# The state layer of an eight-layer kernel: its recurrence inputs summed up spread over the partitions in PSUM, its states read in place, its gate as a tangent, and four row sums in another order

## The chip, the cores and the metric

The kernel runs on one core of one Trainium2 chip, as one launch. The time is device microseconds of that core for the whole program, all eight layers in one go. Kernels are compared by the median of several runs.

## The reference

Sixteen sequences of 256 tokens with 128 features (4096 tokens) go through eight residual layers: cosine attention, a mixture of 160 experts, a gated linear recurrence, the mixture again, the state layer, a feed-forward layer, rotary attention, and the feed-forward layer again. Each is `x = x + f(layernorm(x))`. All is float32. The change is in the fifth, the state layer:

```python
def _L1_attn_a_ref(x, W_in, b_in, conv_w, conv_b, A, C, Dp, W_out, b_out):
    x_and_z = x @ W_in + b_in
    x_proj, z = jnp.split(x_and_z, 2, axis=-1)          # 256 channels each
    xc = causal_conv(x_proj, conv_w)                    # 4 taps for each channel
    x_conv = xc + conv_b
    def step(h, xt):
        h = jnp.tanh(xt @ A + h)                        # 16 states for each sequence
        yt = h @ C.T + Dp * xt
        return (h, yt)
    _, ys = scan(step, 0, x_conv)                       # over the 256 tokens
    return (sigmoid(z) * ys) @ W_out + b_out
```

The scan is the awkward part: a hyperbolic tangent of the sum of this token's input and the last token's state can't be regrouped, so each sequence takes 256 steps one after the other.

## The kernel before, in words

The residual stream `X` stays in SBUF for the whole program as 32 tiles of 128 tokens (partition = token). Every layer goes over it in 8 steps (`STEPS`) of 4 tiles (`TPI`), 512 tokens (`W`), which are two whole sequences. The five engines run instruction streams of their own and meet at semaphores: VectorE (DVE), ScalarE (ACT), TensorE (PE), GpSimd (POOL) and SyncE (SP, which only starts DMAs). Between layers 5, 6, 7 and 8 there is a barrier (`finish`): all compute engines drain and wait for one another. Layers 2, 3, 4 and 5 have none.

The mixture of experts ahead of the state layer leaves its results in DRAM rows (`slot_results`). POOL fetches them back, 8 indirect DMAs for each tile (L1779), into a ring `GATHERED` of four tile places; DVE adds them into `X`, 8 weighted additions for each tile (`sum_rows`, L1749). Tile t+4 is fetched only when tile t has been added. The second half of the tiles (16 to 31) is fetched and added while the state layer already works on the first half, so `mamba_vector` carries these 16 tile sums between its own work; `front(i)` makes sure that the four tiles of step i have been summed.

The state layer (`mamba_*`, lines 832 to 1016) goes, for each step i:
- `front`: DVE takes mean and variance (L573, L577), ACT the square root (`deviations`, L177, which needs its own activation table), DVE the reciprocal (L181) and the normalised rows `XN` (L590), PE transposes them (L602), ACT copies them to `XT` (L934).
- PE multiplies by `W_in` (L993, four matmuls of 128x512), ACT adds the bias to the first half (`XP`, L938) and takes the sigmoid of the second (`Z`, L941).
- DVE does the four taps of the convolution into `XCS` (`convolve`, L900 and L902, 8 instructions).
- ACT copies it into `XC` for the whole layer (L943). PE multiplies by `A` to 16 rows x 512 columns in PSUM bank 5 (L998), and ACT copies that to `U16` (L945), on 16 partitions.

The recurrence (`recur`) works on 8 sequences at once, a group g: 8 sequences x 16 states are 128 partitions, and each token is one ACT instruction on a column of 128x1 (L955, L952 for the first), whose bias is the column before. To bring `U16` from 16 partitions to 128, SP starts 8 small DMAs for each group (`spread`, L973); to bring the states back to 16 partitions for the multiplication by `C`, another 8 (`collect`, L978). Group 0 (steps 0 to 3) is done in four parts of 64 tokens, one behind each of ACT's steps 4 to 7; group 1 follows behind step 7 in one go.

The output (`output(i)`): PE multiplies the states by `C` (L1003, 2 matmuls with 16 rows and 512 columns), DVE adds `D * XC` (L914), multiplies by the gate (L917) and adds the bias to `X` (L919), PE multiplies by `W_out` (L1010, 8 matmuls), DVE adds the result to `X` (L923). The outputs of group 0 run beside the recurrence of group 1; those of group 1 come after it, then the barrier.

The feed-forward layer behind it takes a sigmoid too (L790), inside a hardware loop of 7 rounds and once after it. Loads of activation tables are put in by the compiler, in the program's order, ahead of each function that the table in place doesn't have.

## Time and profile before

| | us |
|---|---|
| median of 3 runs | 2880.16 |
| lowest, highest | 2865.74, 2882.03 |
| the profiled execution, whole time | 2874.02 |
| its span, from first to last instruction | 2872.2 |
| state layer, from its first DVE instruction (1772.36) to the first of the next layer (2169.56) | 397.2 |

Busy shares of the span: PE 60%, DVE 49%, ACT 34%, POOL 38%. The mean clock that TensorE was granted is 0.723 of full speed. The page's first lines give such shares for the whole program; they say little about one layer. For this change the timeline of the state layer, engine by engine, is what is read: each row has a start time from the span's start, how long the row's instructions took together, the engine, the line, what is written from what, how many instructions, and in brackets how long the engine stood idle before it and what ended the wait. "PEld" are weight loads of TensorE.

### The profile page before, as it was taken

To read this page: it belongs to the slowest core of one execution; us is meant where nothing else is said; L and a number is where in the kernel's file an instruction comes from. 1 tells how busy PE (TensorE), PEld (TensorE's weight loads), DVE (VectorE), ACT (ScalarE), POOL (GpSimd) and SP (SyncE) were. 2 spreads that over 40 slices of the span, in tenths; PEclk is the share of its full clock that TensorE was granted. 3 is DMA by queue.
4 is the path that set the end of the run, shared out by engine and by line. 5 is a ranking of instruction groups with operands and counts; after the bars stand their busy time and mean duration, and the time that the engine had idled before them with its cause. 6 is when DMAs were issued, how large, how long until landed. Compare 5 with 4: busy or idle time off the path is not lost.

```text
span 2872.2 us, 40719 instructions
## 1 busy us (share of the span) xinstructions
PE 1731.2 (60%) x13716; PEld 1131.0 (39%) x13716; DVE 1404.3 (49%) x3650; ACT 970.4 (34%) x1719; POOL 1077.8 (38%) x1177
## 2 busy tenths in 40 slices
PE   4765424777676453465676766422426488888965
PEld 2544313555454232243555544100214334554543
DVE  3648833222434677676222444633215466766644
ACT  3651102333233321321332333356842223443342
POOL 2100777743751774765743762770001200000000
PEclk9985556888877655656887887655555568998985
DMA  8990116998996111115998996110000000000001
GB/s 234 327 388 23 48 51 207 320 315 273 324 289 216 52 52 46 51 57 171 321 318 274 327 308 202 50 52 2 4 2 0 0 1 1 1 1 1 1 1 30
DMA packets 294225, 383.68 MB, mean 134 GB/s; under 512 B 70816, under 2 KB 163696, under 8 KB 293872
## 3 DMA queue, kind: packets, MB, share of 16 engines
q1 hardware_dynamic: 177280, 160.91, 17.8%
q10 hardware_dynamic: 83984, 153.13, 15.4%
q0 software_dynamic: 32768, 67.17, 7.3%
q8 instruction: 108, 1.77, 0.2%
q14 instruction: 85, 0.70, 0.1%
HBM read 231.64 MB, written 175.11 MB: 142 GB/s over the span
## 4 chain that ended last, share of the span: by engine, by line
PE 38%; DVE 17%; DMA 13%; ACT 11%; issue 9%; POOL 6%; SPq 4%; DVEq 0%; ACTq 0%; POOLq 0%
DMA arena<-expert_blocks 11%; ACT arena L955 5%; PE psum L1984 5%; PE psum L1974 5%; POOL slot_rows L1768 4%; PE psum L448 3%; PE psum L1947 3%; SPq L1866 3%; PE psum L1347 2%; PE psum L1328 2%; PE psum L432 2%; PE psum L993 1%; PE psum L427 1%; ACT arena L1210 1%; PE psum L815 1%
## 5 line engine op out<-in xcount | busy, mean ns | idle before, releaser
L1779 POOL DMA_INDIRECT arena<-slot_results,SLOTS x512 | 492.3, 962 | 429.9 <-DMA slot_results<-arena 239.0
L1768 POOL DMA_INDIRECT slot_rows<-arena,SLOTS x512 | 512.0, 1000 | 332.4 <-issue 332.4
L1738 DVE COPY arena<-psum 128x512 f32<-128x512 f32 x288 | 197.2, 690 | 632.3 <-PE psum L1984 615.6
L1974 PE MATMUL psum<-arena 128*64 128x128 f32 x2304 | 233.0, 334 | 229.7 <-DMA arena<-expert_blocks 208.0
L1822 ACT ACTIVATE arena<-psum 128x512 f32<-128x512 f32 x288 | 172.0, 597 | 475.7 <-PE psum L1947 435.8
L169 POOL TENSOR_SCALAR rstd<-mv 128x4 f32<-128x4 f32 x32 | 6.2, 195 | 774.6 <-DVE mv L577 774.1
L1947 PE MATMUL psum<-ident,arena 128*128 128x128 f32 x1152 | 224.7, 328 | 72.7 <-DMA arena<-slot_rows 72.1
L1974 PEld LDWEIGHTS psum<-arena 128*64 128x64 f32 x2304 | 148.8, 163 | 296.6 <-DMA arena<-expert_blocks 226.3
L1984 PE MATMUL psum<-arena 64*128 64x128 f32 x2304 | 249.0, 345 | 7.3 <-DVE arena L1738 7.2
L1984 PEld LDWEIGHTS psum<-arena 64*128 64x128 f32 x2304 | 186.2, 226 | 70.4 <-issue 69.7
L1829 ACT ACTIVATE arena<-psum 128x256 f32<-128x256 f32 x288 | 110.6, 384 | 271.7 <-PE psum L1974 268.9
L1749 DVE SCALAR_TENSOR_TENSOR X<-arena,WEIGHTS,X 128x128 f32<-128x128 f32 x512 | 180.1, 352 | 41.0 <-DMA arena<-slot_results,SLOTS 25.1
L1947 PEld LDWEIGHTS psum<-ident,arena 128*128 128x128 f32 x1152 | 145.8, 163 | 117.0 <-issue 80.9
L955 ACT ACTIVATE arena<-arena 128x1 f32<-128x1 f32 x510 | 150.0, 294 | 16.6
L602 PE MATMUL psum<-ident,XN 128*128 128x128 f32 x192 | 45.3, 382 | 174.3 <-DVE XN L590 169.9
L1101 DVE TENSOR_REDUCE arena<-psum 128x1 f32<-128x128 f32 x256 | 74.1, 289 | 101.5 <-PE psum L1347 96.7
L1210 ACT ACTIVATE arena<-psum 128x1536 f32<-128x1536 f32 x64 | 92.8, 1450 | 80.1 <-PE psum L432 80.1
L602 PEld LDWEIGHTS psum<-ident,XN 128*128 128x128 f32 x192 | 34.0, 201 | 204.9 <-issue 193.4
L1102 DVE TENSOR_REDUCE arena<-psum 128x1 f32<-128x256 f32 x256 | 105.8, 413 | 0.0
L448 PE MATMUL psum<-arena 128*32 128x256 f32 (+1 forms) x1536 | 93.5, 349 | 8.6 <-ACT arena L1210 5.3
L427 PE MATMUL psum<-arena 51*128 51x256 bf16 (+1 forms) x384 | 64.7, 285 | 40.3 <-ACT arena L349 22.7
L448 PE MATMUL psum<-arena,ones 128*32 128x256 f32 (+1 forms) x1536 | 88.7, 335 | 0.0
(245 smaller groups left out, 3132.8 us busy)
## 6 DMA issues: line engine op xcount, KB each, us to landing
arena<-slot_rows ACTq DMA_DIRECT2D x288, 256.0 KB
slot_results<-arena ACTq DMA_DIRECT2D x288, 256.0 KB
arena<-expert_blocks SPq DMA_DIRECT2D x512, 96.0 KB
arena<-own_blocks SPq DMA_DIRECT2D x160, 256.0 KB
slot_rows<-zeros SPq DMA_DIRECT2D x2, 18432.0 KB, 79.5
own_blocks<-in_expert_w SPq DMA_DIRECT2D x4, 2560.0 KB, 22.6
slot_rows<-arena,SLOTS POOLq DMA_INDIRECT x512, 2.2
arena<-slot_results,SLOTS POOLq DMA_INDIRECT x512
```

Source lines behind the costliest of these rows:

```text
L448: mm = pe.matmul(psum[32 * r:32 * r + 32, 3, 256 * half + lo:256 * half + hi], ones4[:, head_of(n, r) % 4, :] if half else vp(kt, head_of( ...
L955: act.activation(H[:, g, t:t + 1], U[:, g, t:t + 1], ACT.Tanh, bias=H[:, g, t - 1:t]).then_inc(m_h[g], 1)
L1210: act.activation(PR2[:, g % 2], psum[:, 4:8, 0:384], ACT.Exp, scale=DH ** -0.5).then_inc(r_exp.sem, 1)
L1738: dve.tensor_copy(YSB[:, p].rearrange("p (c h) d -> p h c d", h=2), psum[:, first:first + 2, 0:256].rearrange("p h (c d) -> p h c d", c=2) ...
L1749: dve.scalar_tensor_tensor(X[:, t, :], GATHERED[:, j, k], WEIGHTS[:, t, k:k + 1], X[:, t, :], ALU.mult, ALU.add).then_inc(g_sum.sem, 1)
L1768: pool.indirect_dma_start(out=slot_rows[h], out_offset=bass.IndirectOffsetOnAxis(ap=slots_of(t, k), axis=0), in_=XNH[:, t], in_offset=None ...
L1779: pool.indirect_dma_start(out=GATHERED[:, t % TPI, k], out_offset=None, in_=slot_results[h], in_offset=bass.IndirectOffsetOnAxis(ap=slots_ ...
L1822: act.activation(XSBT[:, g % UNROLL], psum[:, g % 2, :], ACT.Copy).then_inc(c_xt.sem, 1)
L1829: act.activation(HEB[:, g % 2], psum[:, 2 + 5 * (g % 2), 0:256], ACT.Silu).then_inc(c_he.sem, 1)
L1947: mm = pe.transpose(psum[:, p % 2, P * q:P * q + P], XSB[:, p, q], ident[:])
L1974: mm = pe.matmul(psum[lo:lo + INTER, 2 + 5 * (p % 2), o:o + P], gate_of(g, q), XSBT[:, p, P * q:P * q + P], start=True, stop=True, skip_gr ...
L1984: mm = pe.matmul(psum[:, 3 + 2 * (p % 2) + q % 2, c:c + P], HEB[lo:lo + INTER, p % 2, c:c + P], down_of(g, q), start=True, stop=True, skip ...
```

## The change

Seven edits, all in the state layer.

1. The multiplication by `A` uses a wide stationary matrix. `A_AT[:, q, e, :]` is 128x128, zero but for the 16 columns of sequence q. Four matmuls for each step (2 sequences x 2 channel halves, 256 columns each) add into one PSUM bank for each group, banks 5 and 6, so that the inputs of 8 sequences come out on 128 partitions. `U16`, its copy and `spread` go.
2. ACT copies 128x256 from PSUM to `U` once for each group, in `recur`, ahead of the first token.
3. `C_AT` is the same for `C`: 128 rows with the 16 of sequence q filled, loaded by 8 DMAs from DRAM. PE multiplies it with `H` where it lies. `H16` and `collect` go; PE waits on the recurrence's own semaphore.
4. DVE clears and fills these matrices (`spread_out`) ahead of `front(0)`.
5. The gate: `sigmoid(z) = (1 + tanh(z/2)) / 2`. ACT takes the tangent with scale 0.5 and half the bias (`B_HALF`); DVE multiplies by `1 + Z` in one instruction, and the last addition scales by 0.5.
6. The 16 tile sums stand elsewhere: steps 0 to 3 have one each, behind the convolution; steps 4 to 6 have four each, two ahead of it and two behind.
7. Group 0's recurrence is in parts of 64, 96 and 96 tokens behind ACT's steps 4, 5 and 6; step 7 has none. PE's loops are written out.

```diff
-        m_ct = weight("m_ct", [STATE, E2, P])
-        U16 = view([STATE, NSEQ, SEQ])
+        HALF = NSEQ // 2
+        A_AT = view([P, HALF, E2, P])
+        C_AT = view([P, HALF, E2, P])
+        B_HALF = view([P, 2 * E2])
...
             def convolve(i):
-                dve.wait_ge(m_u_ps.sem, m_u_ps.before(0, i))
+                if i:
+                    dve.wait_ge(m_u_ps.sem, m_u_ps.before(0, i))
...
+            def spread_out():
+                dve.memset(C_AT, 0.0).then_inc(m_at, 1)
+                dve.memset(A_AT, 0.0).then_inc(m_at, 1)
+                dve.tensor_scalar(B_HALF, b_in[:], 0.5, None, ALU.mult).then_inc(m_at, 1)
+                dve.wait_ge(m_at, 2)
+                for q in range(HALF):
+                    dve.tensor_copy(A_AT[:, q, :, STATE * q:STATE * q + STATE], m_a[:]).then_inc(m_at, 1)
+            spread_out()
             front(0)
-            for i in range(STEPS - 2):
-                step(i, [TILES // 2 + 2 * i], [TILES // 2 + 2 * i + 1])
-            step(STEPS - 2, [TILES - 4, TILES - 3], [TILES - 2, TILES - 1])
+            for i in range(HSTEPS):
+                step(i, [], [TILES // 2 + i])
+            for i in range(HSTEPS, STEPS - 1):
+                step(i, [TPI * i + TPI, TPI * i + TPI + 1], [TPI * i + TPI + 2, TPI * i + TPI + 3])
...
-                    dve.tensor_tensor(ym(e), ym(e), Z[:, e, bass.ds(i * W, W)], ALU.mult).then_inc(m_ym.sem, 1)
+                    dve.scalar_tensor_tensor(ym(e), Z[:, e, bass.ds(i * W, W)], 1.0, ym(e), ALU.add, ALU.mult).then_inc(m_ym.sem, 1)
...
-                    act.activation(Z[:, e, bass.ds(i * W, W)], psum[:, 1 + E2 + e, :], ACT.Sigmoid, bias=b_in[:, E2 + e:E2 + e + 1]).then_inc(m_xp.sem, 1)
+                    act.activation(Z[:, e, bass.ds(i * W, W)], psum[:, 1 + E2 + e, :], ACT.Tanh, scale=0.5, bias=B_HALF[:, E2 + e:E2 + e + 1]).then_inc(m_xp.sem, 1)
...
-                act.wait_ge(m_u_ps.sem, m_u_ps.at(0, i))
-                act.activation(U16[:, bass.ds(i * 2, 2), :], psum[0:STATE, 5, :].rearrange("p (b q) -> p b q", b=2), ACT.Copy).then_inc(m_u.sem, 1)
...
                     if t == 0:
-                        act.wait_ge(m_spread, 16 * HALF * (g + 1))
+                        act.wait_ge(m_u_ps.sem, m_u_ps.at(0, HSTEPS * g + HSTEPS - 1))
+                        act.activation(U[:, g, :], psum[:, 5 + g, 0:SEQ], ACT.Copy).then_inc(m_h[g], 1)
+                        act.wait_ge(m_h[g], 1)
...
-            for k in range(STEPS // 2):
-                step(STEPS // 2 + k)
-                recur(0, part * k, part * k + part)
+            for k, steps in enumerate((64, 96, 96)):
+                step(HSTEPS + k)
+                recur(0, t, t + steps)
+                t += steps
+            step(STEPS - 1)
             recur(1, 0, SEQ)
...
+            sp.wait_ge(m_at, 1)
+            for q in range(HALF):
+                sp.dma_start(C_AT[STATE * q:STATE * q + STATE, q], a["m_ct"]).then_inc(m_ct, 16)
...
-                for e in range(E2):
-                    mm = pe.matmul(psum[0:STATE, 5, :], m_a[:, e, :], XCS[:, e].rearrange("p b q -> p (b q)"), start=(e == 0), stop=(e == E2 - 1))
+                for b in range(2):
+                    q = 2 * (i % HSTEPS) + b
+                    for e in range(E2):
+                        mm = pe.matmul(psum[:, 5 + i // HSTEPS, 0:SEQ], A_AT[:, q, e, :], XCS[:, e, b, :], start=(q == e == 0),
+                                       stop=(q == HALF - 1 and e == E2 - 1), skip_group_check=True)
...
                 for e in range(E2):
-                    mm = pe.matmul(psum[:, 1 + e, :], m_ct[:, e, :], H16[:, bass.ds(i * 2, 2), :].rearrange("p b q -> p (b q)"), start=True, stop=True)
+                    for b in range(2):
+                        mm = pe.matmul(psum[:, 1 + e, SEQ * b:SEQ * b + SEQ], C_AT[:, 2 * (i % HSTEPS) + b, e, :], H[:, i // HSTEPS, :],
+                                       start=True, stop=True, skip_group_check=True)
...
+            pe.wait_ge(m_ct, 16 * HALF)
+            pe.wait_ge(m_xp.sem, m_xp.end(0))
             for g in range(2):
-                pe.wait_ge(m_gather, 16 * HALF * (g + 1))
+                pe.wait_ge(m_h[g], SEQ + 1)
```

The first place that the prediction speaks of is DVE at the start of the state layer. Before, from the memset of `XP`'s margin (L872) to the first tile sum behind the convolution:

```order
L872 MEMSET arena 128x4x3
L573 BN_STATS stats<-X 128x6 x4
L577 BN_AGGR mv<-stats 128x2 x4
L181 RECIPROCAL rstd<-rstd 128x4
L590 TENSOR_SCALAR XN<-X,mv,rstd 128x128 x4
L1749 SCALAR_TENSOR_TENSOR X<-arena,WEIGHTS,X 128x128 x8
L900 TENSOR_SCALAR arena<-arena,w_conv_w,w_conv_b 128x512 x2
L902 SCALAR_TENSOR_TENSOR arena<-arena,w_conv_w 128x512 x6
L1749 SCALAR_TENSOR_TENSOR X<-arena,WEIGHTS,X 128x128 x8
```

And in the changed kernel, whose lines are some 8 further down (its L901, L903 and L1757 are L900, L902 and L1749 of before):

```order
L872 MEMSET arena 128x4x3
L907 MEMSET arena 128x2048
L908 MEMSET arena 128x2048
L909 TENSOR_SCALAR arena<-w_b_in 128x4
L912 COPY arena<-w_m_a 128x2x16 x8
L573 BN_STATS stats<-X 128x6 x4
L577 BN_AGGR mv<-stats 128x2 x4
L181 RECIPROCAL rstd<-rstd 128x4
L590 TENSOR_SCALAR XN<-X,mv,rstd 128x128 x4
L901 TENSOR_SCALAR arena<-arena,w_conv_w,w_conv_b 128x512 x2
L903 SCALAR_TENSOR_TENSOR arena<-arena,w_conv_w 128x512 x6
L1757 SCALAR_TENSOR_TENSOR X<-arena,WEIGHTS,X 128x128 x8
```

Eleven instructions (L907 to L912) have come ahead of the first `front`, and the tile sum that stood between `XN` and the convolution is gone; its tile is now summed behind the convolution.

The second place is ACT from its last but one step to the end of the layer, with the semaphores that it waits for (`m_u_ps`: PE's multiplication by `A` is done; `m_spread`: a spreading DMA has landed; `m_h0` and `m_h1`: the state before). Before:

```order
L177 ACT_TABLE_LOAD
L177 ACTIVATE rstd<-mv,ln_eps 128x4 [waits f_mv]
L934 ACTIVATE XT<-psum 128x512 [waits m_in,f_xt_ps]
L938 ACTIVATE arena<-psum,w_b_in 128x2x256 [waits m_conv,m_in]
L938 ACTIVATE arena<-psum,w_b_in 128x2x256
L941 ACT_TABLE_LOAD
L941 ACTIVATE arena<-psum,w_b_in 128x512 x2
L943 ACTIVATE arena<-arena 128x2x512 [waits m_conv]
L945 ACTIVATE arena<-psum 16x512 [waits m_u_ps]
L955 ACTIVATE arena<-arena 128x1 [waits m_h0] x64
L952 ACTIVATE arena<-arena 128x1 [waits m_spread]
L955 ACTIVATE arena<-arena 128x1 [waits m_h1] x255
```

And in the changed kernel, from the same square root on:

```order
L177 ACT_TABLE_LOAD
L177 ACTIVATE rstd<-mv,ln_eps 128x4 [waits f_mv]
L947 ACTIVATE XT<-psum 128x512 [waits m_in,f_xt_ps]
L951 ACTIVATE arena<-psum,w_b_in 128x2x256 [waits m_conv,m_in]
L951 ACTIVATE arena<-psum,w_b_in 128x2x256
L954 ACT_TABLE_LOAD
L954 ACTIVATE arena<-psum,arena 128x512 x2
L956 ACTIVATE arena<-arena 128x2x512 [waits m_conv]
L963 ACTIVATE arena<-psum 128x256 [waits m_u_ps]
L965 ACTIVATE arena<-arena 128x1 [waits m_h1]
L968 ACTIVATE arena<-arena 128x1 [waits m_h1] x255
```

The copy on 16 rows with its wait for PE is gone from every step, no recurrence stands behind the last step, and a copy of 128x256 that waits for PE stands ahead of group 1's first token.

The third is ACT's first rounds in the feed-forward layer behind, in the changed kernel. The rows between the two of L798 are entered from a hardware loop of 7 rounds (registers and branches stand in them too):

```order
L798 UNCONDITIONAL_BRANCH
L798 ISA
L788 REGISTER_ALU [waits h_rk]
L789 ISA [waits h_mul]
L790 ACT_TABLE_LOAD
L790 ACTIVATE arena<-psum 128x512 [waits h_link]
L775 REGISTER_ALU
L776 ISA [waits f_xt_ps]
L777 ACTIVATE arena<-psum 128x2x256 [waits h_mix]
L784 ACTIVATE arena<-arena,one_minus_mu 128x512 [waits h_rk,f_xt]
L784 ACTIVATE arena<-arena,one_minus_mu 128x512
L798 REGISTER_ALU
```

Before, the same loop had no table load in the feed-forward layer behind the state layer, and had it in the last layer of the program, behind the rotary attention.

## Rows read from the trace of the kernel before

**Rows 1.** The chain that ended last, 1740 to 2200 us, shares by line (the row ends there)

```profile
by line: ACT arena L955 33.4%; issue 9.7%; PE psum L993 8.8%; DVE arena L902 5.7%; PE psum L998 5.5%; PE psum L1010 3.3%; PE psum L1003 3.3%; POOL arena L1779 3.0%; PE psum L602 1.9%; DVE XN L590 1.9%; DVE arena L900 1.7%; ACT L177 1.7%; AC
```

**Rows 2.** Stretches: us, busy PE, PEld, DVE, ACT, POOL (instructions), PEclk, DMA share, GB/s

```profile
1884.00:2037.00 153.00, 34.25 (x52) 10.35 (x52) 42.56 (x120) 99.68 (x290) 40.84 (x43) 0.56 0.07 19
...
2262.00:2770.00 508.00, 421.56 (x4504) 234.03 (x4504) 312.47 (x821) 197.41 (x194) 26.55 (x51) 0.85 0.01 1
```

**Rows 3.** Timeline of ACT in the state layer, steps 0, 3, 5, 7 and the recurrence

```profile
1782.96 1.27 ACT L938 ACTIVATE arena<-psum,w_b_in 128x512 f32<-128x512 f32 x2 [5.37 <-PE psum L993]
...
1866.05 1.28 ACT L177 ACT_TABLE_LOAD   x1
1867.35 0.30 ACT L177 ACTIVATE rstd<-mv,ln_eps 128x4 f32<-128x4 f32 x1
...
1926.21 1.06 ACT L943 ACTIVATE arena<-arena 128x1024 f32<-128x1024 f32 x1 [3.00 <-DVE arena L902]
1929.93 0.59 ACT L945 ACTIVATE arena<-psum 16x512 f32<-16x512 f32 x1 [2.67 <-PE psum L998]
1930.42 20.86 ACT L955 ACTIVATE arena<-arena 128x1 f32<-128x1 f32 x64
...
2015.25 0.59 ACT L945 ACTIVATE arena<-psum 16x512 f32<-16x512 f32 x1 [2.67 <-PE psum L998]
...
2036.73 83.29 ACT L955 ACTIVATE arena<-arena 128x1 f32<-128x1 f32 x255
```

**Rows 4.** Timeline of DVE in the state layer, steps 0 and 3

```profile
1784.50 3.10 DVE L1749 SCALAR_TENSOR_TENSOR X<-arena,WEIGHTS,X 128x128 f32<-128x128 f32 x8 [8.87 <-DMA arena<-slot_results,SLOTS]
...
1795.38 3.06 DVE L1749 SCALAR_TENSOR_TENSOR X<-arena,WEIGHTS,X 128x128 f32<-128x128 f32 x8 [2.44 <-DMA arena<-slot_results,SLOTS]
...
1799.37 0.38 DVE L577 BATCH_NORM_AGGREGATE mv<-stats 128x2 f32<-128x6 f32 x4
...
1865.50 0.38 DVE L577 BATCH_NORM_AGGREGATE mv<-stats 128x2 f32<-128x6 f32 x4
```

**Rows 5.** Timeline of PE in the state layer, step 7 and the outputs of group 1

```profile
2011.62 3.59 PE L998 MATMUL psum<-arena,w_m_a 128*16 128x512 f32 x4 [6.92 <-DVE arena L902]
...
2126.63 3.77 PE L1003 MATMUL psum<-arena,w_m_ct 16*128 x4 [43.29 <-DMA arena<-arena]
...
2143.87 3.77 PE L1010 MATMUL psum<-w_m_wo,arena 128*128 128x128 f32 x16 [2.99 <-DVE arena L917]
```

**Rows 6.** Groups by line: busy us, mean ns of one | idle before

```profile
L735 DVE MEMSET arena<- 128x2 f32 x2 | 0.1, 60 | 0.4 <-DVEq L2152 0.4
L2008 DVE MEMSET C<- 128x36 f32 x1 | 0.1, 88 | 0.3 <-DVEq L2152 0.3
L382 POOL MEMSET arena<- 128x2048 f32 x1 | 1.8, 1809 | 14.0 <-DMA mask_qk<-in_mask_qk 14.0
L902 DVE SCALAR_TENSOR_TENSOR arena<-arena,w_conv_w 128x512 f32<-128x512 f32 x48 | 34.0, 749 | 0.8
L917 DVE TENSOR_TENSOR arena<-arena 128x512 f32<-128x512 f32 x16 | 10.3, 684 | 0.0
L1829 ACT ACTIVATE arena<-psum 128x256 f32<-128x256 f32 x288 | 110.6, 384 | 271.7 <-PE psum L1974 268.9
L993 PE MATMUL psum<-XT,w_w_in 128*128 128x512 f32 x64 | 45.4, 874 | 6.4 <-ACT XT L934 6.4
L998 PEld LDWEIGHTS psum<-arena,w_m_a 128*16 128x16 f32 x32 | 3.4, 128 | 77.6 <-issue 77.6
```

**Rows 7.** Timeline of POOL, the last fetch for the tile sums

```profile
1938.68 0.94 POOL L1779 DMA_INDIRECT arena<-slot_results,SLOTS  x1 [0.30 <-issue]
```

**Rows 8.** Timeline of ACT, first and last sigmoid of the two feed-forward layers

```profile
2182.51 0.60 ACT L790 ACTIVATE arena<-psum 128x512 f32<-128x512 f32 x1 [5.03 <-PE psum L816]
...
2252.74 0.60 ACT L790 ACTIVATE arena<-psum 128x512 f32<-128x512 f32 x1 [6.38 <-PE psum L816]
...
2787.18 1.28 ACT L790 ACT_TABLE_LOAD   x1 [5.01 <-PE psum L816]
...
2857.39 0.60 ACT L790 ACTIVATE arena<-psum 128x512 f32<-128x512 f32 x1 [6.32 <-PE psum L816]
```

More of the change, by code:

```diff
@@ L929, in mamba_scalar @@
             act.wait_ge(m_zero, 1)
+            act.wait_ge(m_at, 3)
             def step(i):
@@ L950, in recur @@
                     if t == 0:
[L951 removed]
+                        act.wait_ge(m_u_ps.sem, m_u_ps.at(0, HSTEPS * g + HSTEPS - 1))
+                        act.activation(U[:, g, :], psum[:, 5 + g, 0:SEQ], ACT.Copy).then_inc(m_h[g], 1)
+                        act.wait_ge(m_h[g], 1)
                         act.activation(H[:, g, 0:1], U[:, g, 0:1], ACT.Tanh).then_inc(m_h[g], 1)
                     else:
[L954 removed]
+                        act.wait_ge(m_h[g], t + 1)
                         act.activation(H[:, g, t:t + 1], U[:, g, t:t + 1], ACT.Tanh, bias=H[:, g, t - 1:t]).then_inc(m_h[g], 1)
[L958 removed]
+            with act.Fori(0, HSTEPS) as i:
                 step(i)
[L960 to L963 removed]
+            t = 0
+            for k, steps in enumerate((64, 96, 96)):
[3 more added lines that the diff above has]
+            step(STEPS - 1)
             recur(1, 0, SEQ)
         def mamba_sync(sp, layer):
[L968 to L984 removed]
+            sp.wait_ge(m_at, 1)
+            for q in range(HALF):
+                sp.dma_start(C_AT[STATE * q:STATE * q + STATE, q], a["m_ct"]).then_inc(m_ct, 16)
         def mamba_tensor(pe, layer):
             r = front_run(layer)
[L988 removed]
+            for i in range(STEPS):
                 front_tensor(pe, i, r)
@@ L995, in mamba_tensor @@
                 pe.wait_ge(m_conv.sem, m_conv.at(0, i))
[L996 to L998 removed]
+                pe.wait_ge(m_at, 3 + HALF)
+                for b in range(2):
[3 more added lines that the diff above has]
+                                       stop=(q == HALF - 1 and e == E2 - 1), skip_group_check=True)
                 mm.then_inc(m_u_ps.sem, 1)
@@ L1011, in output @@
                 mm.then_inc(m_out.sem, 1)
+            pe.wait_ge(m_ct, 16 * HALF)
+            pe.wait_ge(m_xp.sem, m_xp.end(0))
             for g in range(2):
-                pe.wait_ge(m_gather, 16 * HALF * (g + 1))
-                with pe.Fori(g * STEPS // 2, (g + 1) * STEPS // 2) as i:
+                pe.wait_ge(m_h[g], SEQ + 1)
+                for i in range(g * HSTEPS, (g + 1) * HSTEPS):
                     output(i)
```

30 lines of the change are left out of this document (4 added, 26 removed).

## The prediction

> **What bounds the kernel now.** I first read the chain of waits over the state layer [rows 1]: a third of it is L955, the 128x1 tangents of the recurrence, and TensorE's matmuls and DVE's convolution follow. So the layer is one serial chain. Then the stretches [rows 2]: in 153 us of steps 4 to 7 ACT is busy for 99.7 and PE for 34, at a granted clock of 0.56 (mostly the 1.2 GHz level), so PE is slow there but rarely late. Then ACT's timeline [rows 3], where the reader should look for the gaps between the copy `XC` (L943) and what follows; DVE's [rows 4], for tile sums that wait for a fetch; PE's [rows 5], for what starts when the last state is there. The 512 tangents themselves (64 in 20.86 us, 0.326 each [rows 3]) are the same number before and after, 167 us in all. The change can only take what stands between them.
>
> **The start of the layer (A).** Eleven DVE instructions come ahead of the first `front`. No row has a large memset on DVE. The two small ones [rows 6], 60 ns for 2 elements and 88 ns for 36, give 0.82 ns per element, so 1.75 us for 2048; two are 3.5. The scaling and 8 copies of 32 elements, about 0.1 each when issued back to back, and one wait make 1.0: 4.5 us later. Ends: at no growth with size (0.09 each) the block costs 1.2; at the convolution's rate, 749 ns for 512, it costs 7.0. POOL's memset of 2048 took 1.81 [rows 6], near my value, which I take.
> Against this, the tile sum ahead of convolution 0 goes. It waited 8.87 us for a fetch and ended at 1787.6 [rows 4], while `XP` was ready at 1784.2 [rows 3]. The convolution took from there to 1792.9 (the next sum started at 1795.38 after 2.44 idle), 5.3 us. Now: `XP` at 1784.2 + 4.5, convolution to 1794.1, one sum of 3.1, statistics 1.3 (from the sum's end at 1798.4 to 1799.75 [rows 4]): variances at 1798.5 instead of 1799.75. A is -1.2, between -4.5 and +1.3.
> The Trainium skill (VectorE: DVE Perf Modes, Zero memsets can be issued as uint32) gives a memset one cycle per element whatever the type, at the 0.96 GHz of its table 2.1 us each; by that rule A would be -0.4. The trace has 0.82 ns per element on sizes too small to settle it.
>
> **Square root without PE (B).** In steps 0 to 3 ACT can load the root's table only after the `U16` copy, which waits for PE. In step 3 the load began at 1866.05 and the root at 1867.35, while the variances were there at 1865.88 [rows 3, 4]: 1.4 us late. Now the load starts right behind `XC`, 3 us before the variances. Step 0 is not such a case (there the variances came last). Three of them make 4.3; in step 3 the statistics now also wait for the tile sum just issued, 0.25 back. B is -4.0. PE's multiplication (3.59 us [rows 5]) then lies beside DVE's sum and statistics (4.4 us) and hides.
>
> **Recurrence behind XC (C, D).** In step 5 `XC` ended at 1927.27, the copy of `U16` began 2.67 later and the first tangent at 1930.42 [rows 3]: 3.15 us. Steps 5 and 6 save it whole. Step 4 puts the copy of 128x256 there, 0.38 us [rows 6] plus some 0.15 of waiting: 2.6. C is -8.9. Step 7 has no recurrence of group 0 behind it any more, so group 1 needs PE's result at once: PE ended at 2015.21, ACT's old copy began at 2015.25 and took 0.5 to the first tangent [rows 3, 5]; the new copy and its extra wait take about 0.6. D is +0.1. The 16 spreading DMAs were hidden (group 1's by 64 tangents), so their removal gives nothing by itself.
>
> **The end (E, F).** The last tangent ended at 2120.02 [rows 3]; PE began the outputs of group 1 at 2126.63 [rows 5], after 8 collecting DMAs. Now it waits for the tangent alone, 0.1 us: E is -6.5. The gate's product becomes an addition and product: 749 against 684 ns [rows 6], two in each of four exposed outputs: F is +0.5. The outputs of group 0 lie under 83 us of tangents [rows 3].
>
> **What is cost at nothing, and its cover.** PE's new matmuls have as many columns as the old ones (1024), with more loads of stationary matrices. L1010 streams 1024 columns with 16 matmul instructions and took 3.77, exactly as L1003 with 4 [rows 5]: more loads cost nothing there. If they were exposed: below. Loading `C_AT` is 8 DMAs early in the layer, needed 250 us later. The moved tile sums: POOL fetches a tile in 8 x (0.94 + 0.30) = 10 us and had finished at 1939.6 [rows 7]; now tile 23 waits for the sum of tile 19 in step 3 (about 1861), and eight more tiles take it to about 1955, while the front of step 7 needs them only when 96 tangents (31 us) behind step 6 are over, near 1990. Two sums (6.1 us) lie ahead of a convolution in steps 4 to 6, in the 8 us in which DVE waits for PE and ACT. That cover is 2 us thick.
>
> **Tables.** The tangent gate has the feed-forward layer behind load the sigmoid's table in each of 7 rounds. The last layer of the program has these loads already [rows 8]: from its first load to its last sigmoid 70.21 us, against 70.23 between the same places of the layer without them. The sigmoid waits behind PE, and DVE needs it later still; cost 0. The Trainium skill speaks against this (ScalarE: Activation LUTs, What ACT_TABLE_LOAD costs): a switch costs 1283 ns and a drain of 1380 ns on top. Its first figure is the row's 1.28; by its sum 7 switches would take 18.6 us and nearly all of the gain. The two stretches of 70.2 say that here they take none.
>
> **The sum.** -1.2 - 4.0 - 8.9 + 0.1 - 6.5 + 0.5 = -20.0 us. The profiled execution took 2874.0 (span 2872.2); with the change 2854.0. It lies 6.2 below the median of 2880.2, whose own sum would be 2860.2. The three runs span 16.3 us, so I take a value between: 2858.
>
> **Rivals.**
> 1. Loads of the table are exposed: 7 x 1.28 = 9.0 us [rows 8]. For: they are in the instruction stream. Against: 70.21 and 70.23. Time 2867, chance 0.04.
> 2. The stationary matrices are exposed, mildly: each of 8 loads costs as much as one of L1010's 16 instructions, 0.24 us, so 1.9 in step 7 and in each of four outputs: +9.5, 2867. For: the old matrix of step 7 had 16 columns, the new has 128. Against: rows 5. Chance 0.08.
> 3. The same mechanism at full price, which ends slower than before. A load of 16 columns took 0.128 us [rows 6]; if 128 columns took eight times as long, 1.0, and nothing covered it, the 8 loads of a step would take 8.2: PE would hold up the next step's transposes by about 5 us in steps 0 to 3 (20), group 1's first tangent by 7.7, and four outputs by four more loads each (16). That is +44, so 24 slower than before: 2902. It outweighs the gain from about 0.5 us a load. Against: 16 loads of 128 columns fit in 3.77 us. Chance 0.03. The Trainium skill (TensorE: Matmul & The Clock Gate, Step-by-step: what each phase is for) has the rule that a load's time goes with its columns and not its rows, but also that the next load runs beside the present matmul; by the first alone this case would hold, and the row of 3.77 bears out the second.
> 4. More than I count. PE's input matmuls (L993) took 45.4 us in 8 steps [rows 6], 5.7 a step, at a clock that is between its two levels: at L998's price, 0.90 an instruction [rows 5], a step would take 7.2, at half that 3.6. They start after other gaps now. All at the high level would save 17, all at the low level cost 12; a part of either, with A at its cheap end, gives about 2848. Chance 0.08.
> 5. The change does less than it says: DVE becomes what is late in steps 4 to 6 (the 2 us of cover fail), or a fetch comes late: +3 to +8, 2863. Chance 0.05.
>
> The forecast has 0.72. A measurement of this kernel tells about 1% from no change, 29 us. Faster than that needs rival 4 or a low draw: 0.18. Slower than that is rival 3 for the most part: 0.03. The range, 2843 to 2872, holds the forecast with the runs' own spread, rivals 1, 2 and 5 and most of 4; it leaves rival 3 out.
>
> **What would show it.** In the changed profile: from the layer's first memset to the next layer's about 377 us; two DVE memsets of 1.7 to 2.2; no idle time of ACT ahead of the roots but for DVE; the first tangent of steps 5 and 6 within 0.2 us of `XC`'s end; the first output of group 1 within 0.3 us of the last tangent; the same 70 us in both feed-forward layers. I am wrong if the layer gives less than 12 us or more than 27, if the multiplication by `A` takes over 4.5 us, or if another layer moves by more than 5 us.

## The result, and the profile after

The changed kernel took 2842.74 us (median of 4 runs, 2837.24 to 2850.27), the kernel before beside it 2873.81 (4 runs, 2865.74 to 2882.03). The ratio is 0.9887, with a 95% interval of 0.9845 to 0.993: faster by 1.1%. The forecast was 2858 with a range of 2843 to 2872, so the time lies 0.3 us under the range, by less than the runs scatter. The sum had promised 20.0 us; the two profiled executions differ by 30.2 in their spans (2872.2 and 2842.0).

From the state layer's first memset (128x12) to that of the next layer (128x2) it was 397.2 us and is 368.5: 28.7 of the 30.2. The layer begins 0.8 later, and what follows it is 2.3 shorter (702.6 and 700.4), 2.1 of it in the next feed-forward layer. Inside the layer the terms can be read at the starts of the normalised tiles (`XN`) and at the last tangent, all counted from the layer's start. The changed kernel does 64 more tangents of group 0 ahead of step 7 (0.326 us each); their 20.9 us are taken off in its row for step 7, since it saves them later.

| us from the layer's start | before | after | difference | term (predicted) |
|---|---|---|---|---|
| `XN` of step 1 | 28.0 | 28.5 | +0.4 | A +0.4 (-1.2) |
| `XN` of step 4 | 95.6 | 91.1 | -4.5 | B -4.9 (-4.0) |
| `XN` of step 7 | 224.1 | 210.6 | -13.4 | C -8.9 (-8.9) |
| last tangent ends | 347.7 | 334.3 | -13.3 | D +0.1 (+0.1) |
| first output of group 1 | 354.3 | 334.4 | -19.9 | E -6.6 (-6.5) |
| next layer | 397.2 | 368.5 | -28.7 | F -8.9 (+0.5) |

The differences are taken from the unrounded times. Up to the first output the sum holds within 0.6 us (-19.9; predicted -20.5). The missing 9 us are in the four outputs of group 1. ACT's timeline after answers to [rows 3]:

```profile
1860.29 1.28 ACT L177 ACT_TABLE_LOAD   x1
1863.64 0.30 ACT L177 ACTIVATE rstd<-mv,ln_eps 128x4 f32<-128x4 f32 x1 [2.07 <-DVE mv L577]
...
1919.75 1.06 ACT L956 ACTIVATE arena<-arena 128x1024 f32<-128x1024 f32 x1 [2.94 <-DVE arena L903]
1920.71 31.32 ACT L968 ACTIVATE arena<-arena 128x1 f32<-128x1 f32 x96
...
2023.57 0.38 ACT L963 ACTIVATE arena<-psum 128x256 f32<-128x256 f32 x1 [2.78 <-PE psum L1001]
2023.98 0.20 ACT L965 ACTIVATE arena<-arena 128x1 f32<-128x1 f32 x1
2024.22 83.30 ACT L968 ACTIVATE arena<-arena 128x1 f32<-128x1 f32 x255
```

The root's table is loaded right behind `XC` (L956 ends at 1860.3) and the root now waits 2.07 us for DVE's statistics alone: term B. In step 5 the first tangent follows `XC` in the same instant, where 3.15 us lay between them: term C. Group 1 still waits 2.78 for PE, as before: term D.

DVE's timeline after answers to [rows 4]:

```profile
1773.62 1.76 DVE L907 MEMSET arena<- 128x2048 f32 x1 [0.39 <-issue]
1775.76 1.76 DVE L908 MEMSET arena<- 128x2048 f32 x1 [0.38 <-issue]
1777.56 0.79 DVE L912 COPY arena<-w_m_a 128x32 f32<-128x32 f32 x8
...
1791.32 1.03 DVE L901 TENSOR_SCALAR arena<-arena,w_conv_w,w_conv_b 128x512 f32<-128x512 f32 x2 [9.90 <-ACT arena L951]
...
2112.94 1.28 DVE L929 SCALAR_TENSOR_TENSOR arena<-arena 128x512 f32<-128x512 f32 x2
```

A memset of 2048 takes 1.76 us (1.75 was worked out from the small ones), but 0.39 and 0.38 of issue stand ahead of the two, and the first `XN` starts 7.1 us into the layer instead of 2.2: the block costs 5.0 and not 4.5. The gate's two products take 1.28 together; their mean of 684 ns is that of L917 [rows 6], not the 749 of L902 that term F used.

PE's timeline after, step 7's multiplication by `A` and the outputs of group 1, beside [rows 5] (each of these float32 matmuls stands in the profile as two, so the 8 of L1016 are x16):

```profile
2019.75 3.78 PE L1001 MATMUL psum<-arena 128*128 128x256 f32 x8 [6.85 <-DVE arena L903]
2107.57 3.78 PE L1008 MATMUL psum<-arena 128*128 128x256 f32 x8 [52.30 <-ACT arena L968]
2114.28 3.78 PE L1016 MATMUL psum<-w_m_wo,arena 128*128 128x128 f32 x16 [2.92 <-DVE arena L929]
2117.85 2.97 PE L1008 MATMUL psum<-arena 128*128 128x256 f32 x8
2123.74 3.52 PE L1016 MATMUL psum<-w_m_wo,arena 128*128 128x128 f32 x16 [2.92 <-DVE arena L929]
2127.10 1.89 PE L1008 MATMUL psum<-arena 128*128 128x256 f32 x8
2131.91 2.05 PE L1016 MATMUL psum<-w_m_wo,arena 128*128 128x128 f32 x16 [2.93 <-DVE arena L929]
2133.80 1.89 PE L1008 MATMUL psum<-arena 128*128 128x256 f32 x8
2138.62 2.05 PE L1016 MATMUL psum<-w_m_wo,arena 128*128 128x128 f32 x16 [2.93 <-DVE arena L929]
```

The first row of the outputs starts 0.05 us behind the last tangent (term E) and takes 3.78, as the first one did before (3.77 [rows 5]); the last four rows take half of that. The pauses for DVE ahead of L1016 hardly differ (2.92 and 2.93, before 2.99). L1016 is the unchanged L1010 of before, so a halving of its time points at TensorE's clock, and the windows show it. Before, group 1's outputs:

```profile
2126.00:2170.00 44.00, 30.00 (x80) 18.60 (x80) 16.04 (x28) 0.00 (x0) 0.00 (x0) 0.50 0.00 0
```

After, the same outputs:

```profile
2107.00:2142.00 35.00, 21.40 (x96) 17.96 (x96) 15.96 (x28) 0.48 (x2) 0.00 (x0) 0.77 0.00 0
```

The granted clock (the third number from the end) was 0.50, the level of 1.2 GHz, through all of them; now it is 0.77, so the level of 2.4 GHz is reached in their course. PE is busy for 21.40 us instead of 30.00, which is 8.6 of the 8.9 of term F. What differs on PE is the multiplication by `C` (L1003, now L1008): it used to read 16 partitions and now reads 128.

### The profile page after: what moved, and what is told of

Read it like the earlier page. It is cut to its first block, busy times and chain, and to the rows that moved or that the text cites. A ratio compares the mean times of both kernels' runs of the same rounds, so it can differ in the third digit from the quotient of the medians.

```text
span 2842.0 us, 40748 instructions
## 1 busy us (share of the span) xinstructions
PE 1709.7 (60%) x13780; PEld 1142.8 (40%) x13780; DVE 1407.7 (50%) x3661; ACT 974.7 (34%) x1720; POOL 1076.1 (38%) x1177
## 4 chain that ended last, share of the span: by engine, by line
PE 38%; DVE 18%; DMA 13%; ACT 11%; issue 9%; POOL 6%; SPq 4%; DVEq 0%; ACTq 0%; POOLq 0%
DMA arena<-expert_blocks 11%; ACT arena L968 5%; PE psum L1992 5%; PE psum L1982 5%; POOL slot_rows L1776 4%; PE psum L448 3%; SPq L1874 3%; PE psum L1955 3%; PE psum L1355 2%; PE psum L994 2%; PE psum L1336 2%; PE psum L432 2%; PE psum L427 1%; ACT arena L1218 1%; DVE X L1757 1%
## 5 line engine op out<-in xcount | busy, mean ns | idle before, releaser
L1757 DVE SCALAR_TENSOR_TENSOR X<-arena,WEIGHTS,X 128x128 f32<-128x128 f32 x512 | 179.5, 352 | 23.1 <-DMA arena<-slot_results,SLOTS 7.3
L602 PE MATMUL psum<-ident,XN 128*128 128x128 f32 x192 | 44.0, 373 | 183.9 <-DVE XN L590 167.2
L602 PEld LDWEIGHTS psum<-ident,XN 128*128 128x128 f32 x192 | 33.1, 197 | 206.7 <-DVE XN L590 109.8
```

The source lines that it names most:

```text
L1757: dve.scalar_tensor_tensor(X[:, t, :], GATHERED[:, j, k], WEIGHTS[:, t, k:k + 1], X[:, t, :], ALU.mult, ALU.add).then_inc(g_sum.sem, 1)
```

## The experiments

Theory 1 is that the 128 rows of the new multiplication by `C` raise the clock. The rivals are the written-out loop, the start close behind the tangents, and the other gate. A third possibility is chance, the moment at which the outputs fall. The runs stand on three chips, one for each of the three groups below. Each ratio is to the kernel before on the same chip; lengths of the layer come from one profiled execution of each kernel.

### First chip: what raises the clock

The kernel before took 2880.85 us here (16 runs, 2871.18 to 2889.68).

**The changed kernel, with 16 rows read in the multiplication by `C`.**

```diff
-  mm = pe.matmul(..., C_AT[:, 2 * (i % HSTEPS) + b, e, :], H[:, i // HSTEPS, :],
+  mm = pe.matmul(..., C_AT[0:STATE, 2 * (i % HSTEPS) + b, e, :], H[0:STATE, i // HSTEPS, :],
```

> The changed kernel, but the multiplication by C reads only the first 16 of the 128 rows of C_AT and H (so most sequences get the output of the wrong states: 112 of 128 rows of that product are left out); columns, instruction counts and everything else as they are. Theory 1 (rows: TensorE's granted clock rises in the outputs because its matmuls now use all 128 rows): the four outputs of group 1 stay at the 1.2 GHz level, 10.2 to 10.5 us apart as before, the stretch from the first output to the next layer takes 42 to 43 us instead of 34.0, the whole kernel about 9 us more than the changed one. Theory 2 (the written-out loop or the four matmuls in place of two keep TensorE busier): the stretch stays at 34 us. Theory 3 (chance of the moment): anything between, and group 0's outputs differ from group 1's.

Measured: 2858.79 us (7 runs), ratio 0.9918 (0.9888 to 0.9947). The layer took 376.8 us instead of 368.4, and the `XN` starts are those of the changed kernel within 0.3, so the difference lies in the outputs: 42.7 us from the last tangent to the next layer, instead of 34.1. PE's timeline, first and last output of group 1:

```profile
2104.41 3.78 PE L1008 MATMUL psum<-arena 16*128 16x256 f32 x8 [43.78 <-ACT arena L968]
...
2135.65 3.78 PE L1008 MATMUL psum<-arena 16*128 16x256 f32 x8
...
2142.35 3.78 PE L1016 MATMUL psum<-w_m_wo,arena 128*128 128x128 f32 x16 [2.92 <-DVE arena L929]
```

And the window over them:

```profile
2104.00:2148.00 44.00, 30.03 (x96) 23.90 (x96) 16.50 (x30) 0.32 (x2) 0.00 (x0) 0.50 0.00 0
```

The program, its instructions, their order, their columns and their loads are the same; only the rows differ. All rows take 3.78 and the clock stays at 0.50. Loop, start and gate are as in the changed kernel and bring nothing without the rows. One thing goes with the rows: the first 16 rows of `C_AT` are filled for one sequence in eight and zero for the rest, so most of these products are zero, and not those of the wrong states as the expectation says. Zeros don't tell the levels apart: before, all 16 rows are filled and the clock is at 0.50, and in the changed kernel 112 of the 128 rows are zero and it is at 0.77.

**The kernel before, with 128 rows.** The other way round: only that line of before is replaced by a matmul of equal columns that reads 128 rows, and a wait on `XC` goes with it.

```diff
-  mm = pe.matmul(psum[:, 1 + e, :], m_ct[:, e, :], H16[:, bass.ds(i * 2, 2), :]..., start=True, stop=True)
+  mm = pe.matmul(psum[:, 1 + e, :], w_in[:, e, :], XC[:, e, bass.ds(i * W, W)], start=True, stop=True)
...
+  pe.wait_ge(m_xc.sem, m_xc.end(0))
```

> The kernel before, but the two matmuls of the multiplication by C read a stationary matrix and moving rows of 128 rows (the input weights and the convolved inputs) instead of 16; the multiplication by C itself is left out, and the waits for the collecting DMAs stay. Loops and instruction counts as before. Theory 1 (rows): the outputs of group 1 speed up as in the changed kernel, the stretch from the first output to the next layer takes 34 to 36 us instead of 42.8. Theory 2 (loop form or more matmuls): it stays at 42 to 43. Theory 3 (chance): between.

Measured: 2872.35 us (10 runs), ratio 0.9973 (0.9955 to 0.9991), the layer 387.3 instead of 397.2. PE's timeline, group 1, its first two outputs:

```profile
2138.80 3.69 PE L1003 MATMUL psum<-arena,w_w_in 128*128 x4 [47.43 <-DMA arena<-arena]
2145.49 3.62 PE L1010 MATMUL psum<-w_m_wo,arena 128*128 128x128 f32 x16 [3.00 <-DVE arena L917]
2148.90 1.98 PE L1003 MATMUL psum<-arena,w_w_in 128*128 x4
2153.88 2.05 PE L1010 MATMUL psum<-w_m_wo,arena 128*128 128x128 f32 x16 [3.00 <-DVE arena L917]
```

And the window:

```profile
2138.00:2171.00 33.00, 18.66 (x80) 12.06 (x80) 16.18 (x29) 0.00 (x0) 0.00 (x0) 0.88 0.00 0
```

From the first output to the next layer it took 31.6 us instead of 42.9, with the loop, the sigmoid, the collecting DMAs and the pause of 6.6 us behind the tangents all left in place. So more rows are enough in the kernel before, and without them the changed kernel loses the gain. The wide multiplication by `A` is no rival either: the kernel with 16 rows has it and stays at 0.50, and this one does not have it and is at 0.88. The mean clock over the whole program, which is known for every run, says the same: 0.727 to 0.732 in the 10 runs here against 0.713 to 0.727 in 16 of the kernel before, and 0.716 to 0.728 in the 7 runs with 16 rows against 0.733 to 0.737 in the 4 of the changed kernel with late memsets (below), all on this chip. Why the clock came one output earlier here than in the changed kernel (0.88 against 0.77) is not known.

**The kernel before, with the output loop written out.**

```diff
-  with pe.Fori(g * STEPS // 2, (g + 1) * STEPS // 2) as i:
+  for i in range(g * STEPS // 2, (g + 1) * STEPS // 2):
```

> The kernel before with the output loop of TensorE written out (8 outputs, no hardware loop), nothing else. Theory 1 (rows): nothing changes, 42 to 43 us from the first output of group 1 to the next layer. Theory 2 (loop form): 34 to 38 us.

One run: 2868.32 us, with the layer at 396.2 and the outputs at 40.9 instead of 42.9. The window has a clock of 0.54:

```profile
2130.00:2172.00 42.00, 28.23 (x80) 18.09 (x80) 16.44 (x30) 0.00 (x0) 0.00 (x0) 0.54 0.00 0
```

One multiplication by `C` took 1.98 us, and the matmuls behind it 3.78 again: the clock rose once and did not stay. The kernel before has one such row too, in the outputs of group 0 (1.98 at 2053.65), which lie under the tangents. So 40.9 lies between the two theories' ranges; the loop's form is worth at most these 2 us and is not the cause of the 9.

**Chance of the moment.** Fourteen traces, on all chips, can be set side by side. From the first output of group 1 to the next layer the three kernels that read 16 rows take 42.9, 42.7 and 40.9 us, and the eleven that read 128 rows take 31.3 to 36.8; five of these, the changed kernel and four others, agree within 0.1 us at 34.1. Chance moves the rise by an output or two, and no trace with 128 rows lacks it. Group 0's outputs, hidden under the tangents, rise as well: in the window from 2023 to 2056 us the changed kernel's clock is 0.82, and with 16 rows (2020 to 2063) 0.54.

**The memsets out of the way.** The changed kernel, with `front(0)` first and `spread_out` behind it, in DVE's wait for the first `XP`; only the scaling of `B_HALF` stays ahead, and the waits of DVE, ACT and SP are numbered anew.

```diff
+  dve.tensor_scalar(B_HALF, b_in[:], 0.5, None, ALU.mult).then_inc(m_at, 1)
-  spread_out()
   front(0)
+  spread_out()
```

> The changed kernel with the two large memsets and the eight copies moved behind the first front, where DVE waits 9.9 us for ACT; only the scaling of the bias stays ahead. My reading of the profile (the block lies on the path and costs 5.1 us, gaps included): the first XN starts about 5.0 us earlier and the kernel is about 5 us faster than the changed one. Rival (the fetch of tile 16 is what is late then): the tile sum behind convolution 0 waits for its fetch, and only 1 to 3 us stay.

Measured: 2841.94 us (4 runs), ratio 0.9856 (0.982 to 0.9891). The layer is 6.1 shorter (362.3), `XN` of step 1 starts at 23.1 instead of 28.5. DVE's timeline at the start:

```profile
1780.65 1.12 DVE L590 TENSOR_SCALAR XN<-X,mv,rstd 128x128 f32<-128x128 f32 x4
1782.14 1.76 DVE L907 MEMSET arena<- 128x2048 f32 x1 [0.38 <-issue]
...
1791.01 1.12 DVE L901 TENSOR_SCALAR arena<-arena,w_conv_w,w_conv_b 128x512 f32<-128x512 f32 x2 [4.13 <-ACT arena L951]
```

The block now lies beside PE's and ACT's work, and DVE still waits 4.13 us. Of the 5.4 us by which `XN` of step 1 comes earlier, 4.8 are the block and most of the rest step 0's input matmuls (5.79 instead of 6.44). The whole time is not told apart from the changed kernel's 2842.74; the layer is.

### Second chip: four runs of which only the outputs can be read

Here every kernel took some 640 us longer (before: 3519.45, 11 runs), with long waits that the profile puts down to no engine of this core, as in this row of ACT's timeline (sigmoid kernel):

```profile
2431.20 1.26 ACT L951 ACTIVATE arena<-psum,w_b_in 128x512 f32<-128x512 f32 x2 [16.44 <-remote]
```

The layer took 411 to 438 us in the four of them, so nothing of its length is used. The outputs of group 1 had no such pauses.

**The gate as a sigmoid.**

```diff
-  ACT.Tanh, scale=0.5, bias=B_HALF[...]
+  ACT.Sigmoid, bias=b_in[...]
-  dve.scalar_tensor_tensor(ym(e), Z[...], 1.0, ym(e), ALU.add, ALU.mult)
+  dve.tensor_tensor(ym(e), ym(e), Z[...], ALU.mult)
...
-  dve.scalar_tensor_tensor(xs, psum[:, 3, :], 0.5, xs, ALU.mult, ALU.add)
+  dve.tensor_tensor(xs, psum[:, 3, :], xs, ALU.add)
```

> The changed kernel with the gate as a sigmoid again (products as before). My term F (the combined addition and product costs 65 ns more, two in each exposed output): the layer 0.5 us shorter. The changed profile already speaks for the rival, that it costs nothing (L929 took 1.28 us for two, as L917 did): 0.0 +- 0.2. The table loads in the feed-forward layer behind go: from its first sigmoid to its last 70 +- 1 us with or without; the rival that they are exposed would have it 9 us shorter. The gate is no rival for the faster outputs: their stretch stays at 34 us.

One run, 3499.75 us. The clock still rises: 31.4 us from the last tangent to the next layer, with outputs 8.3, 6.7 and 6.7 apart (by the starts of DVE's first instruction in each). So the gate is not the cause either. In the feed-forward layer behind, the sigmoids have no loads between them here and take 70.21 us. The 34 us expected for the stretch was missed by 2.6; the kernels below show that it moves by more than that on this chip without an edit to the outputs.

**Six needless matmuls beside the last 32 tangents**, meant to have the clock up before the first output.

```diff
   pe.wait_ge(m_h[g], ...)
+  if g: pe.wait_ge(m_h[g], SEQ + 1 - 32); busy(6)   # 128x512, 128 rows each
```

> The changed kernel with six needless matmuls (128 rows, 512 columns, into the free PSUM bank 7) on TensorE beside the last 32 tangents of group 1, so that it is at work when the outputs begin. Theory 1 (the outputs are paced by TensorE's clock, and what it does just before decides the clock): the four outputs follow at 6.7 us each, the stretch from the last tangent to the next layer falls from 34.1 to 27 to 29 us. Rival (the third and fourth output are fast for another reason, such as code that has to be fetched first): the first two stay at 9.5 and 8.2.

Measured: 3505.61 us (8 runs), ratio 0.9965 (0.9947 to 0.9984), but the stretch is 31.3 us; 27 to 29 was expected. They were over 3.3 us before the last tangent, and the first output took 3.56 again. A miss. Without such matmuls the stretch on this chip is 31.4 (sigmoid gate), 34.1 (sums in the old order) and 36.9 (wait put back), so that 31.3 shows neither a gain nor that there was none.

**Tile sums in the order of before, and the wait for PE put back**, each alone; both were run again on the third chip, where their edits stand.

> The changed kernel with the tile sums in the order of before. My term A said that taking tile 16's sum away from ahead of convolution 0 was worth 3.3 us and the wait of the next 2.4. Rival, from the changed profile: with the memsets ahead the inputs come at 1791.2, when the fetch of tile 16 has long landed (1784.5 before), and the sum fits into DVE's wait of 9.9 us, so the order is worth nothing next to the memsets: the layer within 1 us of 368.5. By my term it would be 3 to 5 us longer.

> The changed kernel, but ACT waits again in every step for the multiplication by A and then does a copy of 16 rows x 512 columns (of other data, into a spare place). Terms B and C (ACT's wait for PE was on the path): the roots of steps 1 to 4 come 1.4 us later each, the recurrences behind steps 4, 5 and 6 3.2 us later each, 14 to 16 us in all, layer 383 to 385. Rival (the gain of those steps came from a faster TensorE): under 5 us.

One run each: 3489.41 and 3534.57 us, with layers of 411.0 and 438.4. Neither answers its question. What can be read are the outputs, in which neither kernel differs from the changed one: 34.1 and 36.9 us from the last tangent to the next layer.

### Third chip: the terms of the sum

The kernel before took 2887.7 us here (7 runs).

**The changed kernel again**, as the yardstick.

> The changed kernel itself, to have it beside the others on one chip. The last four runs fell on a chip where every kernel takes some 640 us more and the fetches of the tile sums come late. Expected where fetches are as in the first profile: layer 368 +- 3 us, stretch from the last tangent to the next layer 31 to 34. If the fetches are slow here too: the layer is longer, with DVE waiting for fetches in steps 1 to 6.

2851.4 us (4 runs), ratio 0.9852 (0.9812 to 0.9892); the layer 368.1, from the last tangent on 34.1. The layer repeats within 0.4 us, while its start moves by 9 (1773.2 and 1782.5), as much as the two spans differ (2842.0 and 2850.9). Between these two executions the scatter lies ahead of the layer; the layer's length is the sharper measure. This chip's 2851.4 would have lain inside the range; but the gain over the kernel before, 36.3 us, is further still from the sum's 20. What the expectation says of late fetches on the second chip was a wrong reading: of all tile sums in the four layers there, one has its wait put down to a fetch, 3.81 us in the kernel with the sums in the old order.

**The wait for PE and a copy put back** (terms B and C together). ACT waits in each step for the multiplication by `A` and copies 16 rows, as it did before.

```diff
+  act.wait_ge(m_u_ps.sem, m_u_ps.at(0, i))
+  act.activation(SPARE, XT[0:STATE, :], ACT.Copy).then_inc(m_spare, 1)
```

> As r7_wait, on another chip and beside r9_after: ACT waits in every step for the multiplication by A and copies 16 rows. Terms B and C: the layer 14 to 16 us longer than r9_after's (roots of steps 1 to 4 by 1.4 each, recurrences behind steps 4 to 6 by 3.2 each). Rival (a faster TensorE made the gain of those steps): under 5.

One run, 2854.68 us; the layer 383.3, 15.2 more than the changed kernel: 5.2 up to `XN` of step 4 (term B) and 10.0 from there to step 7 (term C), and next to nothing behind it. ACT's timeline in step 5 has the old gap back:

```profile
1923.99 1.06 ACT L958 ACTIVATE arena<-arena 128x1024 f32<-128x1024 f32 x1 [3.06 <-DVE arena L905]
1927.83 0.63 ACT L960 ACTIVATE arena<-XT 16x512 f32<-16x512 f32 x1 [2.78 <-PE psum L1005]
1928.37 6.82 ACT L972 ACTIVATE arena<-arena 128x1 f32<-128x1 f32 x21
```

The changed kernel's B and C were 13.9 together: they are this wait with its copy.

**Tile sums in the order of before.**

```diff
-  for i in range(HSTEPS): step(i, [], [TILES // 2 + i])
-  for i in range(HSTEPS, STEPS - 1): step(i, [...two...], [...two...])
+  for i in range(STEPS - 2): step(i, [TILES // 2 + 2 * i], [TILES // 2 + 2 * i + 1])
+  step(STEPS - 2, [TILES - 4, TILES - 3], [TILES - 2, TILES - 1])
```

> As r6_sums, on another chip and beside r9_after: the tile sums in the order of before. Where fetches are fast: within 1 us of r9_after's layer (the sum of tile 16 fits in DVE's wait), against 3 to 5 longer by my term A. Where they are slow: the order of before waits for the fetch of tile 17 and 19 early, the new order for tiles 24 to 31 late; which is shorter I can't say from the profile.

One run, 2858.9 us; the layer 368.8, which is 0.7 more. DVE's timeline in step 0:

```profile
1800.10 3.11 DVE L1756 SCALAR_TENSOR_TENSOR X<-arena,WEIGHTS,X 128x128 f32<-128x128 f32 x8 [3.81 <-DMA arena<-slot_results,SLOTS]
1806.31 1.05 DVE L901 TENSOR_SCALAR arena<-arena,w_conv_w,w_conv_b 128x512 f32<-128x512 f32 x2 [3.10 <-ACT arena L950]
```

The sum lies 3.10 us clear of the convolution: with the memsets in front, `XP` comes late anyway, so where the sums stand is worth 0.7 us at most.

**Both kinds of cover together**: the late memsets, and needless matmuls ahead of steps 5 to 7 (10 each, beside the last 28 tangents) and ahead of group 1's outputs (9).

```diff
+  if i > HSTEPS: pe.wait_ge(m_h[0], 1 + (64, 160, 256)[i - HSTEPS - 1] - 28); busy(10)
   front_tensor(i)
...
+  if g: pe.wait_ge(m_h[g], SEQ + 1 - 32); busy(9)
```

> The changed kernel with the memsets and copies behind the first front, and with needless matmuls of 128 rows (bank 7) on TensorE where it would idle: 10 beside the last 28 tangents of each part of group 0, 9 beside the last 32 of group 1. Theory 1 (TensorE's clock paces the input matmuls and the outputs): against the changed kernel 5 to 6 us from the memsets, the input matmuls of steps 5 to 7 fall from 6.2, 6.7 and 5.2 us to under 4.5 each (4 to 6 us in all), the outputs of group 1 follow at 6.7 each (4 to 6 us): 13 to 18 us. Rival (the clock falls again in the 3 us between the last needless matmul and the transposes): only the memsets' 5 to 6 and perhaps the outputs.

Measured: 2843.03 us (4 runs), ratio 0.9851 (0.9821 to 0.9881); the layer 356.7, 11.4 less than the changed kernel, where 13 to 18 was expected. By `XN` of step 5 it was 4.8 ahead (the memsets), by `XN` of step 7 11.2. PE's timeline, step 5 and the first and one later output:

```profile
1893.55 11.59 PE L991 MATMUL psum<-w_w_in 128*128 128x512 f32 x20 [9.25 <-ACT arena L968]
1905.85 0.66 PE L602 MATMUL psum<-ident,XN 128*128 128x128 f32 x4 [0.71 <-DVE XN L590]
1907.20 3.70 PE L1001 MATMUL psum<-XT,w_w_in 128*128 128x512 f32 x8 [0.69 <-ACT XT L947]
...
2091.21 10.90 PE L1028 MATMUL psum<-w_w_in 128*128 128x512 f32 x18 [41.81 <-ACT arena L968]
2101.94 1.89 PE L1015 MATMUL psum<-arena 128*128 128x256 f32 x8
...
2121.82 3.78 PE L1023 MATMUL psum<-w_m_wo,arena 128*128 128x128 f32 x16 [2.93 <-DVE arena L929]
```

The needless matmuls are L991 and L1028. With PE kept at work to 0.71 us ahead of the transposes (L602), the input multiplication of step 5 took 3.70 us instead of 6.19, and step 6's, with a gap of 0.40, 3.70 instead of 6.68; step 7's, with a gap of 1.83, took 5.28 and gained nothing. The first multiplication by `C` took 1.89 instead of 3.78, but the clock fell again later (L1023 took 3.78 in the third output), and the outputs took 34.3 in all, no less than 34.1. So the gain in steps 5 and 6 was as expected, and those of step 7 and of the outputs did not come. As the shortest layer it is the best version found. Its whole time is not told apart from the changed kernel's 2851.4, since the runs scatter by more than the 11 us.

## Why the prediction was wrong, step by step

**What holds.** B, C, D and E are right in place and within 1.0 us in size, and putting the wait back costs 15.2 us, against the 13.9 of B and C. That C meets its -8.9 to the decimal is partly luck: step by step it is -3.7, -2.3 and -2.9 against the predicted -2.6, -3.15 and -3.15, and the input matmuls of steps 4 to 6 took 0.7 us more together. The table loads cost nothing, as was predicted. After, from its first sigmoid to its last:

```profile
2155.61 0.60 ACT L790 ACTIVATE arena<-psum 128x512 f32<-128x512 f32 x1
2163.88 1.28 ACT L790 ACT_TABLE_LOAD   x1 [5.82 <-PE psum L816]
2165.17 0.60 ACT L790 ACTIVATE arena<-psum 128x512 f32<-128x512 f32 x1
...
2223.71 0.60 ACT L790 ACTIVATE arena<-psum 128x512 f32<-128x512 f32 x1 [6.31 <-PE psum L816]
```

That is 68.1 us with six loads between them and a seventh ahead of the first, against 70.23 without [rows 8], and 69.87 with them in the kernel of 16 rows. With and without loads most rounds take one of two lengths, 9.6 or 10.5 us, and these stretches differ in how many of each they have. The 70.21 of the prediction began at a load and the 70.23 at a sigmoid; from sigmoid to sigmoid the first is 68.9, so the two did not agree as closely as it says; its conclusion stands. Rival 1 (+9.0) is out. The load rows are 1.28 and the sigmoid stands 0.01 behind; the Trainium skill (ScalarE: Activation LUTs, What ACT_TABLE_LOAD costs) has 1380 ns of drain beside the 1283, of which no row here shows any on the path. Rivals 2 and 3 (exposed stationary matrices) are out: eight loads of 128 columns fit in 3.78, and in 1.89 at the higher clock. Rival 5 is out: each convolution of the changed kernel waits for ACT and none for a sum or a fetch, and the order of the sums is worth 0.7.

**The step that failed is F**, and with it the sentence on cover that PE's new matmuls "have as many columns as the old ones". From equal columns I took equal time, 3.77 by [rows 5], and left +0.5 for the gate. The gate costs nothing, and the multiplication by `C` and the untouched output multiplication behind it ran partly at the higher level in the second output and wholly in the third and fourth: -8.9 instead of +0.5. The two runs that change only the rows of that multiplication move the same stretch from 34.1 to 42.7 and from 42.9 to 31.6. F is off by 9.4 us; B adds 0.9 of gain and A 1.6 of loss, which makes the 8.7 between -28.7 and -20.0. By its own signs the prediction is wrong in one place, since the layer gave 28.7 us and more than 27; the multiplication by `A` took 3.78, and the feed-forward layer moved by 2.1, both within their bounds.

**Rival 4** had the mechanism, TensorE's clock, and the sign, but in another place. It put the clock at the input matmuls, 45.4 us before and 47.3 after: these got slower, and 1.3 of that is step 0 (5.12, now 6.44). The rival's 2848 was nearer than the forecast, for a reason that did not occur. [Rows 2] had shown the clock as low where PE is rarely late; the outputs of group 1, where PE is what is waited for, had no window of their own in my reading. It would have shown 0.50 with PE busy for 30.0 of 44 us, so that up to 15 us (an estimate: half of 30.0) stood at risk there.

**A** was -1.2 and is +0.4: the block costs 0.5 more than the 4.5, for the issue ahead of the memsets, and step 0's input matmuls 1.3 more, which is not in the sum. The memset itself was right at 1.76, with some luck, since the 1.75 was drawn from two memsets of 2 and 36 elements; the Trainium skill (VectorE: DVE Perf Modes, Zero memsets can be issued as uint32) has one cycle per element, an estimate of 2.1 at its 0.96 GHz, and the trace decides for less. The late memsets show that the whole block could be hidden.

**The range** left out the measured time by 0.3 us; what failed is the sum of 20 against 28.7 in the layer. The range was built on the runs' scatter and small rivals; it had no place for a clock that changes on the exposed path, worth 9 us, though [rows 2] showed that both levels occur.

## What to carry to other kernels

When a change replaces a matmul by one that reads more rows, price the stretch at both clock levels, though columns and instructions stay the same; look first at the granted clock of the stretches in which PE is waited for. A wait that keeps an engine from its own next step costs what stands between its end and that step, once per round, and this can be read from the timeline to the microsecond. When runs scatter by 10 us, compare the length of the changed layer between two marks in the profiles; it repeated within 0.4 us in two profiled executions.

## What the runs showed of the hardware that I had not expected

- The same matmuls with the same columns, loads and pauses leave TensorE's granted clock over the outputs at 0.50 with 16 rows read, and go with 0.77 with 128. Busy time does not explain it: the first output takes the same 3.78 and 3.78 us with the same pause of 2.92 in both, and from the second on the slower stretch is the busier one (PE 30.03 of 44 us in all, against 21.40 of 35). Sizes between 16 and 128 were not tried, and what inside the chip connects rows and clock is not shown.
- Needless matmuls helped where the real ones followed within a microsecond (3.70 instead of 6.19 us) and left the first output slow when they ended 3.3 us before (3.56). Why the clock rose ahead of the outputs and then fell among them, and whether the gap of 1.83 us is why step 7 gained nothing, stays open.
- Each large DVE memset had 0.37 to 0.39 us of issue ahead of it, at the start of the layer and in the kernel with late memsets alike.
- The second chip took 640 us more for every kernel, with waits of up to 24 us in the layer that the profile puts down to no engine of this core; only stretches without such pauses could be compared.
